# Laying out the input of an LSTM stage: one tile of each graph ahead of the steps, the other three beside the first 64 steps

## The reference, cut to what matters

```
def _layernorm(x, axis=-1, eps=1e-05):
    m = jnp.mean(x, axis=axis, keepdims=True)
    v = jnp.var(x, axis=axis, keepdims=True)
    return (x - m) / jnp.sqrt(v + eps)
...
        x_proj = jnp.einsum('btd,gd->btg', x, W_ih) + b_ih + b_hh
...
        def step(carry, xp):
            h, c = carry
            gates = xp + h @ W_hh.T
            i, f, g, o = jnp.split(gates, 4, axis=-1)
            c = jax.nn.sigmoid(f) * c + jax.nn.sigmoid(i) * jnp.tanh(g)
            h = jax.nn.sigmoid(o) * jnp.tanh(c)
            return ((h, c), h)
...
    x = x + _L0_ffn_ref(_layernorm(x, axis=-1), ...)
```

## Time and profile before

| what | value |
|---|---|
| time, median of 3 runs | 4995.22 us (4994.98 to 4999.32) |
| the profiled execution's own time | 4982.11 us |
| its span in the trace | 4980.0 us |
| busy: PE, DVE, ACT, POOL | 74%, 58%, 40%, 36% |
| LSTM stage in the trace | starts at about 740 us, first step's gates read at 792.77 us |

### The profile page before, as it was taken

How to read it: one execution, slowest core, us unless ns; L and a number is a source line. 1 busy time by engine, 2 the same in 40 slices (tenths; PEclk the granted TensorE clock), 3 DMA queues, 4 the chain that set the end, 5 groups by cost and what they waited for, 6 DMA issues and landing times. The chain is left out here.

```text
span 4980.0 us, 82349 instructions
## 1 busy us (share of the span) xinstructions
PE 3668.2 (74%) x24205; PEld 2239.0 (45%) x24205; DVE 2889.9 (58%) x10948; ACT 1986.3 (40%) x4974; POOL 1803.9 (36%) x2183
## 2 busy tenths in 40 slices
PE   3999985566666569999886766489667777764995
PEld 1333333444444323333364555357455444442663
DVE  5666655555555656666487867622377454543444
ACT  1666652222222236666432255334355433332221
POOL 3444421000000044445262136735545234342445
PEclk9999995555555579999998887699889988885997
DMA  4333319300000043333000022144431000001445
GB/s 125 115 113 103 103 50 419 143 0 0 0 0 0 0 130 106 111 106 95 13 0 1 1 89 76 38 133 148 145 101 52 1 9 14 14 17 45 130 130 162
DMA packets 237330, 378.21 MB, mean 76 GB/s; under 512 B 24832, under 2 KB 157056, under 8 KB 228672
## 3 DMA queue, kind: packets, MB, share of 16 engines
q1 hardware_dynamic: 218688, 337.44, 21.3%
q0 software_dynamic: 18432, 38.31, 2.2%
HBM read 210.70 MB, written 164.95 MB: 75 GB/s over the span
## 5 line engine op out<-in xcount | busy, mean ns | idle before, releaser
L1428 DVE CUSTOM_DVE_ANT_0 mha_seen<-mha_score,mha_mask 128x512 f32<-128x512 f32 x1024 | 686.6, 688 | 456.8 <-PE mha_score L1199 453.8
L1331 ACT ACTIVATE mha_prob<-mha_turned 128x512 f32<-128x512 f32 x1024 | 608.9, 601 | 491.8 <-PE mha_turned L1210 461.5
L1592 PE MATMUL lstm_gates<-lstm_h_part,lstm_w_part 128*128 128x16 f16 x4608 | 277.5, 179 | 338.2 <-DVE lstm_h_part L1779 338.2
L3071 POOL DMA_INDIRECT expert_rows<-expert_y,expert_target x320 | 307.1, 960 | 369.1 <-DVE expert_y L3217 155.4
L1199 PE MATMUL mha_score<-mha_k_rows,mha_q_rows 96*128 96x512 bf16 x1024 | 397.0, 390 | 56.9 <-DVE mha_low L1428 28.4
L1592 PEld LDWEIGHTS lstm_gates<-lstm_h_part,lstm_w_part 128*128 128x128 f16 x4608 | 215.7, 107 | 484.3 <-DVE lstm_h_part L1779 482.2
L1209 PE MATMUL mha_turned<-mha_maskT,core_ident_bf 128*128 128x512 bf16 x1024 | 393.3, 384 | 4.2 <-ACT mha_prob L1331 3.5
L1210 PE MATMUL mha_turned<-mha_q_rows,mha_k_rows 99*128 99x512 bf16 x1024 | 391.4, 382 | 0.0
L1542 POOL TENSOR_TENSOR core_mid<-lstm_hist,lstm_per_unit 128x128 f32 x64 | 29.3, 458 | 876.6 <-DVE lstm_hist L1780 876.6
L879 DVE CUSTOM_DVE_ANT_0 mha_prob<-mha_score,mha_mask 128x384 f32<-128x384 f32 (+3 forms) x256 | 125.0, 488 | 306.6 <-PE mha_score L518 222.2
L690 ACT ACTIVATE mha_prob<-mha_prob,mha_bias 128x384 f32<-128x384 f32 (+3 forms) x256 | 143.6, 561 | 361.3 <-DVE mha_bias L879 344.0
(11 more groups left out here) (559 smaller groups left out, 9055.4 us busy)
## 6 DMA issues: line engine op xcount, KB each, us to landing
routed_rows<-lstm_blank SPq DMA_DIRECT2D x66, 1056.0 KB, 27.0
core_params<-adj SPq DMA_DIRECT2D x32, 1024.0 KB, 5.6
gat_adj_raw<-adj SPq DMA_DIRECT2D x32, 1024.0 KB, 5.4
mha_q_rows<-split_rows SPq DMA_DIRECT2D x64, 384.0 KB, 4.3
mha_k_rows<-split_rows SPq DMA_DIRECT2D x64, 384.0 KB, 5.2
expert_x<-routed_rows SPq DMA_DIRECT2D x80, 264.0 KB
expert_w<-weights SPq DMA_DIRECT2D x80, 256.0 KB
combine_pair<-expert_rows SPq DMA_DIRECT2D x32, 512.0 KB, 4.9
```

Of the source, the lines that this page charges most:

```text
L1331: act.activation(prob[:, n % RING, :], turned[n % 2][:, :], ACT.Exp, scale=-1.0).then_inc(S["prob_ready"], 1)
L1428: dve.tensor_tensor_reduce(seen[n % 2][:, :], score[n % 2][:, :], mask[1 - s][:, t, :], 1.0, 3e38, ALU.add, ALU.min, low[g][:, t, j:j + 1] ...
L1592: return pe.matmul(out, w[:, g * P:(g + 1) * P], h_part[:, part, :], start=False, stop=stop, skip_group_check=True)
L3071: pool.indirect_dma_start(out=core.y_rows[NUMBER][:, :], out_offset=bass.IndirectOffsetOnAxis(ap=target[q][:, t:t + 1], axis=0), in_=y_buf ...
```

## The change

- The 16 first tiles of the graphs (tile 0, steps 0 to 127) are laid out ahead of the steps and ahead of the setup; the 48 others (tiles 1 to 3) in 24 pairs during the first 64 steps.
- Normalising is one VectorE operation for each tile of 128 by 128, with `rstd` and `shift` as two values for each partition. GpSimd's multiplication is gone, and so are VectorE's addition and its copies out of `tpose`.
- Pair i is normalised after steps 0, 2 and 4 of a chunk, turned by TensorE after steps 5, 6 and 7, and copied by ScalarE after the same steps. Three pairs a chunk, eight chunks.
- The first 64 steps are written out on TensorE, VectorE and ScalarE instead of looping.
- Ahead of step 64 TensorE waits for the last of the 24 pairs to be copied.

TensorE's list at the start of the stage, before: `lstm_tpose` is the turned input, `lstm_xn` the normalised one, `lstm_gates` with `lstm_x_and_sums` the input products.

```diff
@@ -1463,7 +1463,7 @@
         m = Mem(nc, ctx, "lstm")
         rstd, shift = m.sb("rstd", [P, B, T]), m.sb("shift", [P, B, T])
         scratch, term = m.sb("scratch", [P, B, T]), m.sb("term", [P, B, T])
-        xn = [m.sb(f"xn{s}", [P, T, D]) for s in range(2)]
+        xn = [m.sb(f"xn{s}", [P, 4, D]) for s in range(4)]
         x_and_sums = m.sb("x_and_sums", [P, LAG * PART + N * B])
         xT = x_and_sums[:, LAG * PART:]
         hT = core.mid[:, :, :, :].rearrange("p b t d -> p (b t d)")
...
@@ -1524,17 +1524,6 @@
         def _(pool):
             pool.memset(blank[:, :], 0.0).then_inc(S["blank_set"], 1)
             pool.memset(x_and_sums[:, 0:LAG * PART], 0.0).then_inc(S["pad_set"], 1)
-            pool.wait_ge(S["stat_done"], STATS[False])
-
-            def normalise(b, s):
-
-                pool.wait_ge(S["xt_in_psum"], b + 1)
-                pool.tensor_tensor(xn[s][:, :, :], core.x_res[:, b], over_features(rstd[:, b]), ALU.mult)\
-                    .then_inc(S["half_mean"], 1)
-
-            with pool.Fori(0, B // 2) as j:
-                for s in range(2):
-                    normalise(j * 2 + s, s)
 
             def save(c, block, i):
 
@@ -1552,7 +1541,13 @@
 
         @block.tensor
         def _(pe):
-            pe.sem_inc(S["xt_in_psum"], 2)
+            for n in range(4):
+                pe.wait_ge(S["xn_ready"], n + 1)
+                if n >= 2:
+                    pe.wait_ge(S["first_taken"], n - 1)
+                for i in range(4):
+                    last = pe.transpose(tpose[n % 2][:, i * P:(i + 1) * P], xn[n][:, i, :], core.ident[:, :])
+                last.then_inc(S["first_turned"], 1)
             pe.wait_ge(core.params_in[k], 16)
             pe.wait_ge(S["widest_found"], 1)
             pe.matmul(gates[0][0:1, 0:P], widest[:, :], core.ident[:, :], start=True, stop=True).then_inc(S["widest_moved"], 1)
@@ -1560,19 +1555,16 @@
             pe.matmul(gates[1][:, 0:1], ones_row[:, :], widest_all[:, :], start=True, stop=True).then_inc(S["widest_moved"], 1)
             pe.wait_ge(S["bias_cut"], 3)
             pe.transpose(logit[0:12, 0:P], bias_parts[:, :], core.ident[:, :]).then_inc(S["bias_moved"], 1)
-
-            def turn(b, s):
-                pe.wait_ge(S["xn_ready"], b + 1)
-                pe.wait_ge(S["xT_act" if s == 0 else "xT_dve"], j + 1)
-                for t in range(T):
-                    last = pe.transpose(tpose[s][:, t * P:(t + 1) * P], xn[s][:, t, :], core.ident[:, :])
-                last.then_inc(S["xt_in_psum"], 1)
-
-            with pe.Fori(0, B // 2) as j:
-                for s in range(2):
-                    turn(j * 2 + s, s)
-            pe.wait_ge(S["xT_act"], B // 2 + 1)
-            pe.wait_ge(S["xT_dve"], B // 2 + 1)
+            pe.wait_ge(S["first_taken"], 4)
+
+            def turn_pair(i):
+
+                pe.wait_ge(S["xn_ready"], 4 + i + 1)
+                if i >= 2:
+                    pe.wait_ge(S["pair_taken"], i - 1)
+                for j in range(2):
+                    last = pe.transpose(tpose[i % 2][:, j * P:(j + 1) * P], xn[i // 2 % 4][:, i % 2 * 2 + j, :], core.ident[:, :])
+                last.then_inc(S["pair_turned"], 1)
 
             def bias(s):
 
@@ -1609,7 +1601,7 @@
                 out = bank[:, i * PART + cut.start:i * PART + cut.stop]
                 return pe.matmul(out, w_lin[:, i, :], hT[:, bass.ds(u * PART + cut.start, PART // 2)], start=True, stop=True)
 
-            def sixteen(it, u, last=False):
+            def sixteen(it, u, last=False, lay_out=False):
 
                 for s in range(2):
                     c = it * 2 + s
@@ -1620,6 +1612,8 @@
                                 bias(1 - s)
                             elif t <= 4:
                                 project(c + 1, 1 - s, t % 4)
+                        if lay_out and t >= C - 3:
+                            turn_pair(c * 3 + t - (C - 3))
                         if u is None:
                             continue
                         if s == 0 and t == 5:
@@ -1636,8 +1630,9 @@
             for n in (1, 2, 3, 0):
                 project(0, 0, n)
             pe.wait_ge(S["w_parts"], 2)
-            with pe.Fori(0, LAG) as it:
-                sixteen(it, None)
+            for it in range(LAG):
+                sixteen(it, None, lay_out=True)
+            pe.wait_ge(S["pair_taken"], 8 * (T - 1))
             sixteen(LAG, 0)
             with pe.Fori(LAG + 1, PARTS - 1) as it:
                 sixteen(it, it - LAG)
@@ -1659,10 +1654,17 @@
 
         @block.scalar
         def _(act):
-            act.sem_inc(S["xT_act"], 1)
-            with act.Fori(0, B // 2) as j:
-                act.wait_ge(S["xt_in_psum"], j * 2 + 1 + 2)
-                act.copy(xT[:, :].rearrange("p (t b) -> p b t", b=B)[:, j * 2, :], tpose[0][:, :]).then_inc(S["xT_act"], 1)
+            turned = lambda t: xT[:, t * P * B:(t + 1) * P * B].rearrange("p (t b) -> p b t", b=B)
+            for n in range(4):
+                act.wait_ge(S["first_turned"], n + 1)
+                act.copy(turned(0)[:, 4 * n:4 * n + 4, :], tpose[n % 2][:, :].rearrange("p (b t) -> p b t", b=4)).then_inc(S["first_taken"], 1)
+
+            def take_pair(i):
+
+                act.wait_ge(S["pair_turned"], i + 1)
+                first = i % 8 * 2
+                act.copy(turned(1 + i // 8)[:, first:first + 2, :], tpose[i % 2][:, 0:2 * P].rearrange("p (b t) -> p b t", b=2))\
+                    .then_inc(S["pair_taken"], 1)
 
             def step(g, s, t):
                 act.wait_ge(S["gates_done"], g + 1)
@@ -1673,7 +1675,12 @@
                 act.wait_ge(S["c_ready"], g + 1)
                 act.activation(tanh_c[:, :], act5[:, 4, :], ACT.Tanh, scale=0.5).then_inc(S["tc_ready"], 1)
 
-            with act.Fori(0, CHUNKS // 2) as it:
+            for c in range(2 * LAG):
+                for t in range(C):
+                    step(c * C + t, c % 2, t)
+                    if t >= C - 3:
+                        take_pair(c * 3 + t - (C - 3))
+            with act.Fori(LAG, CHUNKS // 2) as it:
                 for s in range(2):
                     for t in range(C):
                         step((it * 2 + s) * C + t, s, t)
@@ -1689,7 +1696,28 @@
         @block.vector
         def _(dve):
             rsqrt_stats(dve, S["stat_done"], rstd[:, :, :], shift[:, :, :], core.x_stat, scratch[:, :, :], term[:, :, :], LN_EPS)
-            dve.sem_inc(S["xT_dve"], 1)
+            dve.wait_ge(S["stat_done"], STATS[False])
+            apart(dve, core)
+
+            def normalise(slot, b, t):
+
+                return dve.tensor_scalar(slot, core.x_res[:, b, t, :], rstd[:, b, t:t + 1], shift[:, b, t:t + 1], ALU.mult, ALU.add)
+
+            for n in range(4):
+                for i in range(4):
+                    last = normalise(xn[n][:, i, :], 4 * n + i, 0)
+                last.then_inc(S["xn_ready"], 1)
+
+            def normalise_pair(i):
+
+                if i >= 8:
+                    dve.wait_ge(S["pair_turned"], i - 8 + 1)
+                elif i == 0:
+                    dve.wait_ge(S["first_turned"], 4)
+                for j in range(2):
+                    last = normalise(xn[i // 2 % 4][:, i % 2 * 2 + j, :], i % 8 * 2 + j, 1 + i // 8)
+                last.then_inc(S["xn_ready"], 1)
+
             dve.wait_ge(core.params_in[k], 16)
             setup = Chain(dve, S["w_chain"])
             setup.step(dve.memset(limit[:, :], 0x7F800000))
@@ -1757,14 +1785,6 @@
             dve.memset(act5[:, :, :], 0.0).then_inc(S["h_full"], 1)
             for part, sem in enumerate(("hi_ready", "low_ready")):
                 dve.memset(h_part[:, part, :], 0.0).then_inc(S[sem], 1)
-            with dve.Fori(0, B // 2) as j:
-                for s in range(2):
-                    dve.wait_ge(S["half_mean"], j * 2 + s + 1)
-                    dve.tensor_tensor(xn[s][:, :, :], xn[s][:, :, :], over_features(shift[:, j * 2 + s]), ALU.add)\
-                        .then_inc(S["xn_ready"], 1)
-                dve.wait_ge(S["xt_in_psum"], j * 2 + 2 + 2)
-                dve.tensor_copy(xT[:, :].rearrange("p (t b) -> p b t", b=B)[:, j * 2 + 1, :], tpose[1][:, :])\
-                    .then_inc(S["xT_dve"], 1)
 
             def step(g, s, t):
                 dve.wait_ge(S["tanh_ready"], g + 1)
@@ -1805,12 +1825,14 @@
                     ins = dve.scalar_tensor_tensor(own, sums, both[:, :], own, ALU.mult, ALU.add)
                 ins.then_inc(S["labelled"], 1)
 
-            def sixteen(it, new, old):
+            def sixteen(it, new, old, lay_out=False):
 
                 for s in range(2):
                     dve.wait_ge(S["hist_saved"], it * 2 + s + 1)
                     for t in range(C):
                         step((it * 2 + s) * C + t, s, t)
+                        if lay_out and t in (0, 2, 4):
+                            normalise_pair((it * 2 + s) * 3 + t // 2)
                         n = t if s else t + 2
```

(6 more changed lines are left out.)

## The result

| | before | changed |
|---|---|---|
| median of the runs (4 each) | 4995.1 us | 4963.0 us (4959.97 to 4967.74) |
| ratio to before, 95% interval | | 0.9936 [0.9919, 0.9954] |
| profiled execution, its span | 4980.0 us | 4959.4 us (own time 4961.14) |

The kernel became 32.1 us faster by the medians, 0.64%. Measured again in more rounds it was 0.994 [0.9927, 0.9954], and on another chip 0.9948 [0.9935, 0.9962], where the medians lie 26.3 us apart.

The account below looks back on a forecast made before the run. Bound: the LSTM stage's chain over all engines, with 35.36 us ahead of step 0 in which no step runs. Gains of 31.8 and 0.2 make 32.0 us, so 4995.2 - 32.0 = 4963.2 us; range 4950 to 4973.

Parts of the forecast that it names:

- Sixteen tile operations: VectorE normalising the first tiles ahead of the setup: adds 4.1 us, plus about 0.1 waiting for the statistics.
- w_in: Its four VectorE operations in the setup shrink from 2.04 to 0.64 us without GpSimd beside them: 1.4 us saved.
- Turning and copying the first 16: TensorE and ScalarE work ahead of step 0: costs nothing, hidden by a margin of 2 us.
- First gates: Layout leaves the path ahead of step 0; gates read at 761.0 instead of 792.77 us: 31.8 us gained.
- Pair on VectorE: 24 pairs normalised behind a step's low half: 0.59 us each, fitting the hole, so nothing.
- TensorE: 24 pairs transposed within the steps: some 0.7 us each at half clock, done before the next products, so nothing.
- ScalarE: 24 pair copies behind the cell tanh: 0.6 us each, ending before the next gates, so nothing.
- Step 64: VectorE's loop exit gives back 0.50 us, TensorE's wait for the last copy costs 0.3: 0.2 us gained.
- pairs fit: Rival claimed the opposite: pair work overflows the step, gain shrinking by up to 17.5 us; halfway 4972 us; chance 0.11.
- copies between tanhs: Rival within the steps: late transposes or ScalarE table reloads give 22 us back, 4985 us; chance 0.03.
- written-out code under full transfer engines: Rival in steps 0 to 63: instructions arrive late, 54 us lost against 32 gained, 5017 us; chance 0.04.
- The way from the profiled execution to the median: Whole kernel: median taken to lie 13.1 us above the profiled execution, with the same saving applied to both.

Follow-up runs that it names:

- e11: The changed kernel again, unaltered, on a third chip: 4947.86 us, 0.9948 of the kernel before.
- e3: Kernel before, old loop kept, with VectorE normalising tile by tile and GpSimd's multiplication and VectorE's addition gone: 4989.3 us, 0.9993.
- e8: Changed kernel with a GpSimd multiplication of 128 by 512 beside each of the 24 pairs: steps 0 to 63 in 126.53 us, 13.6 more.
- e5: Changed kernel without the 24 pairs, tiles 1 to 3 set to zero by GpSimd: steps 0 to 63 in 112.58 us against 112.89.
- e6: Changed kernel with each pair normalised twice by VectorE: steps 0 to 63 in 121.18 us, 8.3 more.
- e7: Changed kernel with each pair copied twice by ScalarE: steps 0 to 63 in 113.16 us, 0.3 more.
- e1: The changed kernel again, unaltered, in more rounds: 4960.15 us against 4995.6 for the kernel before, 0.994.
- e9: Changed kernel with part of the setup moved behind steps 1 to 6, last-pair wait behind step 79, saved-chunk wait into the chunk's first step: 4950.71 us, 0.9939.
- e4: Kernel before with only its first 64 steps written out on TensorE, ScalarE and VectorE: 4992.66 us, ratio 1.0.
- e2: Changed kernel with all 64 tiles laid out ahead of the setup and nothing beside the steps: 4972.66 us, 0.9956 of the kernel before.

## Why the prediction was right, step by step

The predicted time was 4963 us, the measured one 4963.0. The mechanism held; the agreement to a fraction of a microsecond is luck. The interval of the ratio leaves room for gains from 23 to 40 us, the same kernel gained 26 us by the medians on another chip (e11), and the stage itself became 31.2 us shorter for the 32.0 of the sum.

1. Sixteen tile operations: 4.19 us for the 4.1 taken from another stage's row, with 0.15 for the wait ahead (0.1).
2. w_in: 0.61 us for the 0.64. The cause, GpSimd beside it, was tested by e3, where the same four operations took 0.61 us with GpSimd's multiplication gone, and the other way round by e8.
3. Turning and copying the first 16: hidden. The fourth group's copy ended at 751.72, 12.2 us behind the stage's start, and TensorE's first small product ran at 750.60, 2.2 us ahead of VectorE's use of it (752.77); the margin was put at 2.
4. First gates: 31.84 us earlier for the 31.8.
5. Pair on VectorE: 0.60 for 0.59, nothing on the path (e5), and what two pairs would exceed the hole by was right to 0.1 us in 8.4 (e6).
6. TensorE: 0.67 for "some 0.7", at half clock as forecast. The pairs lay ready three to five steps ahead (normalised after steps 0, 2, 4, turned after 5, 6, 7), not one to three as I wrote; nothing hung on it.
7. ScalarE: 0.571 for 0.6. The room in this hole was underrated: I held a full 1.03 us to exceed it by 0.15 a step, but two copies with nearly that length passed (e7), since neighbours on ScalarE overlap.
8. Step 64: TensorE's wait cost 0.18, not 0.3 (e1, e9), and VectorE's exit gave 0.41 back, not 0.50. Missed altogether: the first step of each written-out chunk is 0.07 us longer, 0.56 in 64 steps. The three together cost 0.3 us where 0.2 of gain was forecast. That all 512 steps still take 0.1 us less than before is chance: the steps behind step 65 took 0.6 us less in this execution, and they differ by 2.2 us among all traces.

The rivals fell for the reasons weighed: pairs fit (e5), copies between tanhs reload no table, written-out code under full transfer engines runs on (e4). The way from the profiled execution to the median, a constant 13.1 us, was a weak step. The changed kernel's own profiled execution lies 1.9 us under its median, and by the executions' own times the gain would have read 21 instead of 32.

Not foreseen in the prediction was the division of the gain: moving work beside the steps is 12 us, and 20 are there without it (e2), of which 16 are the leaner pipeline; its operation alone gains nothing (e3). Which of the three parts (copies off VectorE, four buffers, groups) carries the 16 was not separated.

## What to carry to other kernels

In a stage bound by a chain over several engines, write down each engine's hole within one period, from the start of the last operation ahead of it to the start of the next, and cost what is to go there by start-to-start pitch; the overflow of VectorE's hole was predicted to 0.1 us in 8.4 that way (e6). Look for the layout work's own circle first: half of this gain came from breaking it (normaliser, turner and copier on three engines, so that the normaliser never waits), and 12 us of 32 from hiding what is left. When one execution's total disagrees with a sum, measure the stage by its own start, since a part that holds an expert stage moved by 10 us between executions on one chip here (772.7 to 782.9), and by more between chips.

## What the runs showed of the hardware

- Written-out code made a chunk's first step 0.07 us longer than a loop of the same code (1.82 or 1.83 in e4 against 1.74 to 1.76 in the kernel before). Moving the lone wait ahead of that step into it took the 0.07 off seven of eight such steps (e9). The loop has the same lone wait and doesn't pay for it; why is open.
- ScalarE's neighbouring copies of 128 by 256 started 0.37 us apart though one takes 0.57 (e7). Writing every sixteenth column costs 0.571 us where a dense copy of this size takes 0.350.
- Two tile operations of VectorE beside one GpSimd operation of 1.04 us took 1.33 us instead of 0.60 and ended 0.34 behind it (e8).
- In e2, where the transposes of the layout went on for 16 us, TensorE's clock rose to full speed (2.4 GHz) during them; in the changed kernel, with sixteen, it stood at half (1.2 GHz, 0.50 from 745 to 751 us). In e2 the windows read as follows, the clock in the third column from the right:

```profile
745.00:753.00 8.00, 6.26 (x27) 4.39 (x28) 8.00 (x32) 5.54 (x6) 0.00 (x0) 0.58 1.01 416
753.00:756.00 3.00, 2.15 (x16) 1.38 (x14) 3.00 (x13) 3.00 (x4) 0.00 (x0) 1.00 1.02 417
...
771.00:780.00 9.00, 5.93 (x75) 4.28 (x76) 4.16 (x30) 2.50 (x15) 0.00 (x0) 0.50 1.01 418
```

TensorE was busy for 6.26 of the 8 us ahead of the stretch at 1.00. Four transposes took 0.63 us there instead of about 1.1, and the steps that followed had half speed again.
